# Block ranks of the first batch alone, K block sums between the tiles, mask fills interleaved: an order change in a two-layer kernel on one core

## The chip, the cores and the metric

The kernel runs as one program on one core of one Trainium2 chip. The time is device microseconds of that core. Before the change the median of three runs is 677.49 us (677.4 to 678.2).

A core has five engines with instruction queues of their own: TensorE (PE), VectorE (DVE), ScalarE (ACT), GpSimd (POOL) and SyncE (SP, which here only starts DMAs). Each works through its queue in order. They are tied together by semaphores alone, which the program sets and waits for by hand; no scheduler reorders anything.

## The reference, cut to what matters

Two layers over x of 4 x 256 tokens of width 256, each `x + attention(layernorm(x)) + ffn(layernorm(x))`. Layer 0 is a latent attention with 16 heads and a mixture of 32 experts. Layer 1, in which the change lies, is a block-sparse attention with 16 heads of width 16 and a low-rank mixture of 8 experts:

```
q, k = rope(x @ Wq.T), rope(x @ Wk.T);  v = x @ Wv.T          # 16 heads of 16
km   = k.reshape(B, 8, 32, H, d).mean(axis=2)                 # mean key of each block of 32 tokens
gate = einsum('bshd,bnhd->bhsn', q, km)                       # a score of each token for each block
gate = where(future, -1e30, gate); gate = where(selfb, 1e30, gate)
sel  = the 4 best blocks of each token and head
p    = softmax(where(sel & causal, q k / sqrt(d), -1e30));  o = rmsnorm(p v);  attn = o @ Wo.T

logits = x @ Wg.T;  rw, sel = top_k(softmax(logits), 2);  rw = rw / rw.sum()
base1, base3 = x @ W1.T, x @ W3.T;  a1, a3 = x @ A1[e].T, x @ A3[e].T   (rank 32, each of 8 experts)
for k in (0, 1):                                              # the two chosen experts e
    x2   = silu(base1 + a1[e] @ B1[e].T) * (base3 + a3[e] @ B3[e].T)
    out += (x2 @ W2.T + (x2 @ A2[e].T) @ B2[e].T) * rw[:, k]
```

## The kernel before, in words

Layer 0 fills the first 345 us or so; after it come layer 1's projections (to 379 us), a stretch of preparation (379 to 401 us), the block attention in 16 quads of four heads (401 to 471 us), and then layer 1's feed-forward, almost all TensorE work, to the end. The tokens lie in 8 tiles of 128 (NT), two tiles to a batch (QT), so batch 0 is tiles 0 and 1.

**Projections.** The 8 tiles of q and k are made feature-major, 128 features by 512 tokens (a bank each), in the order PROJECTED: four K tiles, then four Q tiles. For each, VectorE multiplies the bank with the cosines (L1725) and swaps halves by a shuffle (L1728), and GpSimd multiplies the swapped part with the sines (L913). The two are added on VectorE for a K tile (L1734) and on GpSimd for a Q tile (L916). ScalarE copies v and the router's logits out.

**Preparation.** VectorE sums the finished K tiles over blocks of 32 (L1739, one reduction over all 2048 columns), spreads the sums into `kmean` by a product with a head mask (L1745, twice), then takes the largest router logit and the difference from it (L1751, L1753). ScalarE makes the exponentials (L1181), and VectorE ends the router: sum, reciprocal, product, top 8 and their indices, one-hot rows of the first and second expert (L1776), the shares (L1779). In the meantime TensorE does four "low" fills (low-rank parts of x, L2257), then, once q and `kmean` are there, the block scores (L2246, 16 short matmul pairs into banks 0 and 1), four more "low" fills, and eight "mask" fills (L2261) that turn the one-hot rows, which ScalarE has widened to 32 columns per expert (L1213, `expert_of`), into feature-major masks. ScalarE copies every fill out (L1205).

VectorE then takes the block scores of all four batches from the banks (L1784), adds the forced values (L1787), and ranks the blocks: `compare` (L699) writes for a distance d which block beats the one d places on, 0 or 1 in bf16, and `count` (L708, L710) adds these into `rank` and subtracts them from the other side. Batch 0 is counted on VectorE, the rest (tiles 2 to 7) on GpSimd. For the rest VectorE makes comparisons 1 to 3 ahead of the first quad and 4 to 7 behind it. GpSimd waits for all seven, counts three batches, and only then makes the mask difference `step_maskT` (L933).

**Block attention.** For each quad TensorE makes scores (L2274, L2280), VectorE adds the bias of the ranks and takes the minimum in one instruction per part (`masked_minimum`, L1805), ScalarE makes exponentials (`exponents`, L1222), TensorE turns them (L2290), VectorE and ScalarE copy the turned ones out (`odd_probsT`, L1814; `even_probsT`, L1228), and TensorE multiplies them with v. GpSimd prepares the feed-forward's operands meanwhile.

What sets the order around the change is the order in which the code of each engine is written, and these semaphores: `r1_step` and `r1_own` (router, widened rows), `blk_mm`, `blk_step`, `blk_count` (block scores, first ranks), `rest_beats`, `rest_count` (other batches), `kmean_done`, `qkT_out`, `fill_mm`, `fill_out`.

Of the kernel before, what the change touches and what calls it, by code (L numbers as in the profile page):

```python
# [14 lines left out]
ALU = mybir.AluOpType  # L15
ACT = mybir.ActivationFunctionType
AX = mybir.AxisListType
# [285 lines left out]
def program(nc, t, y):  # L303

    ctx = ExitStack()
    with ctx:
# [505 lines left out]
        def _(pool):  # L812
# [96 lines left out]
            for n, (j, c) in enumerate(PROJECTED):  # L909
                plain, turned_ = (rope_tmp[:, n % 4, k, :] for k in range(2))  # L910
                by_batch = turned_.rearrange("p (b s) -> p b s", s=S)
                pool.wait_ge(rope_mul, 2 * n + 2)
                pool.tensor_tensor(by_batch, by_batch, along(heads_rope[:, 1], (1, CH // S)), ALU.mult).then_inc(rope_add, 1)  # L913
                if n >= K_TILES:
                    pool.wait_ge(rope_add, n + 1)
                    pool.tensor_tensor(qkT[:, j, c * CH:(c + 1) * CH], plain, turned_, ALU.add).then_inc(qkT_out, 1)  # L916
# [15 lines left out]
            pool.wait_ge(fill_out, 16)  # L932
            pool.tensor_tensor(step_maskT, second_maskT, first_maskT, ALU.subtract).then_inc(step_mask, 1)  # L933
# [49 lines left out]
        def _(act):  # L983
# [217 lines left out]
            for n, (what, j, h, c) in enumerate(fills()):  # L1201
                act.wait_ge(fill_mm, n + 1)
                cols = slice(c * CH, (c + 1) * CH)
                dst = {"low": am_step[j][:, h, cols], "mask": (first_maskT, second_maskT)[j][:, h, cols]}[what]
                act.activation(dst, bank[4 + n % 4][:, :], ACT.Copy).then_inc(fill_out, 1)  # L1205
                if n == 3:
                    act.wait_ge(qkT_out, len(PROJECTED) - K_TILES)
                    for G in range(2):
                        for par in range(2):
                            own_queries(G, par)  # L1210
                    for k in range(2):
                        act.wait_ge(r1_step, 8 + 2 * NT + k)
                        act.activation(expert_of[k].rearrange("p t (e r) -> p (t e) r", r=R1),  # L1213
                                       along(one_of[k].rearrange("p t e -> p (t e)"), (2, R1)), ACT.Copy).then_inc(r1_own, 1)
                if n == len(fills()) - 4:
                    own_bias(0)
# [30 lines left out]

            own_bias(1)
# [77 lines left out]
        def _(dve):  # L1326
# [393 lines left out]
            for n in range(len(PROJECTED)):  # L1720
# [17 lines left out]
            dve.wait_ge(kmean_done, K_TILES)  # L1738
            dve.tensor_reduce(kblock, qkT[:, 2:4, :].rearrange("p k (n c) -> p k n c", c=CHUNK), AX.X, ALU.add)\  # L1739
                .then_inc(kmean_done, 1)  # L1740
            dve.wait_ge(kmean_done, K_TILES + 1)
# [7 lines left out]

            dve.wait_ge(v_out, NT)  # L1750
            dve.tensor_reduce(max1, logit1, AX.X, ALU.max).then_inc(r1_step, 1)  # L1751
            dve.wait_ge(r1_step, 1)
            dve.tensor_tensor(logit1, logit1, along(max1, (2, E1)), ALU.subtract).then_inc(r1_sub, 1)  # L1753
# [28 lines left out]
            for i in range(2):  # L1782
                dve.wait_ge(blk_mm, 4 * i + 4)
                dve.tensor_tensor(g_b[:, 2 * i:2 * i + 2, :], bank[i][:, :].rearrange("p (b n) -> p b n", b=2),  # L1784
                                  along(table("keep"), (1, 2)), ALU.mult).then_inc(blk_step, 1)
            dve.wait_ge(blk_step, 2)
            dve.tensor_tensor(g_b, g_b, along(table("force"), (1, B)), ALU.add).then_inc(blk_step, 1)  # L1787
            dve.wait_ge(blk_step, 3)
# [5 lines left out]
            for d in (1, 2, 3):  # L1794
                compare(dve, rest_heads, beats_rest, rest_beats, d)
# [54 lines left out]
            for Q in range(QUADS + 4):  # L1850
# [67 lines left out]
        def _(pe):  # L1918
# [316 lines left out]
            for n, (what, j, h, c) in enumerate(fills()):  # L2235
# [4 lines left out]
                if n == 4:  # L2240
                    pe.wait_ge(rope_mul, 2 * len(PROJECTED))
                    pe.wait_ge(kmean_done, K_TILES + 1 + KD)
# [15 lines left out]
                else:  # L2258
                    pe.wait_ge(r1_own, j + 1)
# [161 lines left out]
            pe.wait_ge(blk_step, 2)  # L2421
# [62 lines left out]
```

## Time and profile before

| what | value |
|---|---|
| median of 3 runs | 677.49 us (677.4 to 678.2) |
| profiled execution | 677.35 us, its span 675.3 us |
| TensorE busy | 652.1 us, 97% |
| VectorE, ScalarE, GpSimd busy | 504.9, 412.8, 304.5 us |
| TensorE clock granted | 1.0 of full speed throughout |

The profiled execution's own time is 2.05 us more than its span, which is what lies around the span. The busy share of TensorE says that it works nearly always, but it is an average over stages with different limits, and in the stretch from 379 to 471 us its matmuls are short and wait for others.

### The profile page before, as it was taken

The numbers are of one execution on the slowest core, as the hardware profiler recorded it, in microseconds if no ns is written. First come the engines' busy times: TensorE is split into PE (matmuls) and PEld (weight loads), VectorE is DVE, ScalarE is ACT, GpSimd is POOL, SyncE is SP. The second block draws the span as 40 slices with busy tenths as digits, with TensorE's granted clock in tenths as the row PEclk, the third lists the DMA queues.
The fourth block names the chain that finished last, engine by engine and source line by source line (L and its number), as shares of the span: only waits on it lengthen the run. The fifth ranks groups of instructions, "written<-read, shape, count | busy, mean of one in ns | idle before, by whom it ended". The sixth has DMA issues, their size and how long they took to land.

```text
span 675.3 us, 13767 instructions
## 1 busy us (share of the span) xinstructions
PE 652.1 (97%) x4724; PEld 570.2 (84%) x4724; DVE 504.9 (75%) x1429; ACT 412.8 (61%) x1076; POOL 304.5 (45%) x305
## 2 busy tenths in 40 slices
PE   5999999999999999999999988999999999999998
PEld 3777888898988889888888765656899999999997
DVE  6797876878778786887698998899577745645444
ACT  3766158888888888888864389998554222222221
POOL 1584146455463746452343818999533700400000
PEclk9999999999999999999999999999999999999999
DMA  8903034445536353344560000301100000000000
GB/s 322 373 2 100 3 113 135 153 123 162 159 117 195 100 180 117 116 138 120 210 272 1 1 0 2 111 2 56 72 1 1 2 17 1 1 17 1 1 17 16
DMA packets 26869, 59.65 MB, mean 88 GB/s; under 512 B 3162, under 2 KB 12764, under 8 KB 26416
## 3 DMA queue, kind: packets, MB, share of 16 engines
q1 hardware_dynamic: 23728, 50.58, 22.8%
q0 software_dynamic: 3072, 8.20, 3.6%
q8 instruction: 38, 0.62, 0.4%
q14 instruction: 31, 0.25, 0.1%
HBM read 48.47 MB, written 10.49 MB: 87 GB/s over the span
## 4 chain that ended last, share of the span: by engine, by line
PE 70%; DVE 17%; ACT 8%; issue 3%; DMA 0%; POOL 0%; ACTq 0%; DVEq 0%
PE bank L2321 10%; PE bank L2066 7%; PE bank L2000 6%; PE bank L2057 5%; PE bank L2372 5%; PE bank L2346 5%; ACT sb L1222 4%; PE bank L2086 4%; PE bank L2077 4%; PE bank L2007 4%; PE bank L2128 3%; PE bank L2388 3%; PE bank L2290 2%; PE bank L1940 2%; PE bank L2219 2%
## 5 line engine op out<-in xcount | busy, mean ns | idle before, releaser
L1085 ACT ACTIVATE sb<-bank,sb 128x256 f32<-128x256 f32 x128 | 59.6, 472 | 38.7 <-DVE sb L1586 37.7
L1289 ACT ACTIVATE h_parts<-sb 128x256 fp32r<-128x256 f32 x56 | 23.4, 418 | 76.7 <-DVE sb L1845 45.5
L2066 PE MATMUL bank<-sb 128*128 128x256 f32 x256 | 66.2, 381 | 0.0
L1586 DVE TENSOR_REDUCE sb<-bank 128x2 f32<-128x512 f32 x64 | 43.7, 683 | 27.0 <-PE bank L2066 26.5
L2321 PE MATMUL bank<-rounded,b_hi 128*128 128x256 f32 x224 | 63.0, 281 | 0.0
L2321 PE MATMUL bank<-rounded,b_lo 128*128 128x256 f32 x224 | 63.0, 281 | 0.0
L2321 PE MATMUL bank<-am_lo,b_hi 128*128 128x256 f32 x224 | 62.9, 281 | 0.0
L845 POOL DMA_INDIRECT expert_out<-sb x32 | 33.1, 1034 | 61.3 <-DVE sb L1528 47.4
L1092 ACT ACTIVATE sb<-sb 128x256 f32<-128x256 f32 x128 | 57.8, 504 | 0.1
L1836 DVE TENSOR_TENSOR sb<-sb,bank 128x256 f32<-128x256 f32 x56 | 23.4, 419 | 44.8 <-ACT sb L1246 44.7
L1246 ACT ACTIVATE sb<-bank 128x256 f32<-128x256 f32 x56 | 21.4, 382 | 53.2 <-PE bank L2321 53.2
L2000 PEld LDWEIGHTS bank<-sb 128*128 128x128 f32 (+1 forms) x384 | 46.0, 186 | 5.7 <-DVE sb L1522 3.8
L839 POOL DMA_INDIRECT sb<-rows_x,sb x32 | 32.8, 1026 | 39.0 <-PE bank L2000 19.6
L2000 PE MATMUL bank<-sb 128*128 128x128 f32 (+1 forms) x384 | 49.4, 278 | 0.8 <-DVE sb L1522 0.8
L1597 DVE TENSOR_TENSOR pt_parts<-bank,pt_parts 128x512 fp32r<-128x512 f32 x64 | 43.7, 683 | 8.6 <-ACT pt_parts L1105 7.8
L2066 PEld LDWEIGHTS bank<-sb 128*128 128x128 f32 x256 | 45.2, 190 | 4.8
L1847 DVE TENSOR_TENSOR h_parts<-sb,h_parts 128x256 fp32r<-128x256 f32 x56 | 28.1, 502 | 27.9 <-ACT h_parts L1289 27.9
L1222 ACT ACTIVATE sb<-sb 128x128 f32<-128x128 f32 (+1 forms) x128 | 46.7, 443 | 0.5 <-DVE sb L1805 0.5
L2086 PE MATMUL bank<-pt_parts,xt_parts 128*128 128x256 f32 x256 | 46.0, 301 | 0.0
L2057 PE MATMUL bank<-rounded 128*128 128x512 f32 x160 | 42.7, 399 | 0.2 <-ACT sb L1114 0.2
L2321 PEld LDWEIGHTS bank<-rounded,b_lo 128*128 128x128 f32 x224 | 42.2, 188 | 0.0
L2321 PEld LDWEIGHTS bank<-rounded,b_hi 128*128 128x128 f32 x224 | 42.2, 188 | 0.0
(326 smaller groups left out, 1949.6 us busy)
## 6 DMA issues: line engine op xcount, KB each, us to landing
sb<-in_w_gate_up SPq DMA_DIRECT2D x32, 368.0 KB, 3.0
sb<-in_w_down SPq DMA_DIRECT2D x32, 256.0 KB, 2.7
sb<-in_w_pair SPq DMA_DIRECT2D x8, 704.0 KB, 4.1
expert_out<-sb SPq DMA_DIRECT2D x1, 4096.0 KB, 23.2
sb<-expert_out SPq DMA_DIRECT2D x8, 512.0 KB, 6.9
sb<-in_w SPq DMA_DIRECT2D x1, 1792.0 KB, 12.6
sb<-in_b SPq DMA_DIRECT2D x1, 1792.0 KB, 7.2
sb<-in_sw_up SPq DMA_DIRECT2D x1, 1536.0 KB, 8.8
```

Of the source, the lines that this page charges most:

```text
L1085: act.activation(probs[:, u % 4, q, :], bank[3 + u % 2][:, q * S:(q + 1) * S], ACT.Exp, scale=-1.0, bias=row_min[:, u % 4, q:q + 1], accum ...
L1092: ins = act.activation(probs[:, slot, q, :], probs[:, slot, q, :], ACT.Copy, scale=row_inv[:, slot, q:q + 1])
L1222: act.activation(probs1[:, n % 4, a:b], masked[:, n % 4, a:b], ACT.Exp, scale=-1.0, bias=row_min[:, n % 4, q:q + 1]).then_inc(bl_exp, 1)
L1586: dve.tensor_reduce(row_min[:, u % 4, :], bank[3 + u % 2][:, :].rearrange("p (q n) -> p q n", q=QT), AX.X, ALU.min).then_inc(at_min, 1)
L1597: dve.tensor_tensor(r(probs_lo[:, u % 2]), bank[5 + u % 2][:, :].rearrange("p (a b) -> p a b", a=QT), probs_hi[:, u % 2], ALU.subtract).th ...
L2000: mm = pe.matmul(bank[1][0:n, to:to + P], w_gu[s][:, k, a:a + n], xeT[s][:, k, :], start=(k == 0), stop=(k == KD - 1))
L2057: mm = pe.matmul(where[:, :], r(w[i][:, cols]), r(q[:, half]), start=(n == 0), stop=(n == len(terms) - 1))
L2066: mm = pe.matmul(bank[3 + u % 2][:, q * S:(q + 1) * S], qb[i][:, h, b * S + q * P:b * S + (q + 1) * P], keys[:, h, b * S:(b + 1) * S], sta ...
L2086: mm = pe.matmul(bank[2 + 5 * h][:, 0:S], r(v_parts[:, QT * b + k, :]), r(part[:, u % 2, k, :]), start=(n == 0), stop=(n == len(terms) - 1))
L2321: mm = pe.matmul(dst, lhs, rhs, start=False, stop=(n == len(terms) - 1), skip_group_check=True)
L2346: pe.matmul(dst, r(w[:, 2 * k + j, :]), r(x[:, k, :]), start=(i + j == 0), stop=False, skip_group_check=True)
L2372: mm = pe.matmul(bank[4 + k][:, h * CW:(h + 1) * CW], r(w[:, rows_]), r(x), start=(f + h + i == 0), stop=(f == NF1 - 1 and i == 2), skip_g ...
```

## The change

Seven edits, all of order:

1. The K block sums are four reductions of 512 columns, one behind each of the last four tiles (`n >= K_TILES`), instead of one of 2048 behind all.
2. The router's largest logit and the difference stand ahead of the two `kmean` products.
3. GpSimd multiplies the last tile's sines directly behind those of the tile before; the last Q tile's sum moves from GpSimd to VectorE, behind the `kmean` products.
4. The second expert's widened rows are made by GpSimd instead of ScalarE, and every mask fill waits for both.
5. The fills are four low, then four times one low and two mask. ScalarE's `own_bias(0)` moves from between the last fills to behind them.
6. VectorE takes batch 0's block scores alone (256 columns), forces, compares and counts them; only then the other batches' scores, their forced values and comparison 1. Comparisons 2 to 4 stand behind quad 0, 5 to 7 behind quad 1.
7. GpSimd waits for batch 0's counts before it spreads the shares, and makes `step_maskT` ahead of the counts of the rest; it no longer waits for all seven comparisons at once, since `count` waits for each.

```diff
@@ fills
-            out = [("low", j, h, c) for j in range(2) for h in range(2) for c in range(TOK // CH)]
-            return out + [("mask", k, h, c) for k in range(2) for h in range(2) for c in range(TOK // CH)]
+            low, mask = ([(what, j, h, c) for j in range(2) for h in range(2) for c in range(TOK // CH)]
+                         for what in ("low", "mask"))
+            return low[0:4] + [fill for i in range(4) for fill in (low[4 + i], mask[2 * i], mask[2 * i + 1])]
@@ GpSimd
+            for n in range(len(PROJECTED) - 2):
+                heads_sine(n)
                 if n >= K_TILES:
+                    queries_sum(n)
+            for n in (len(PROJECTED) - 2, len(PROJECTED) - 1):
+                heads_sine(n)
+            queries_sum(len(PROJECTED) - 2)
...
             pool.wait_ge(qkT_out, len(PROJECTED) - K_TILES)
+            pool.wait_ge(r1_step, 9 + 2 * NT)
+            pool.tensor_copy(expert_of[1].rearrange("p t (e r) -> p (t e) r", r=R1),
+                             along(one_of[1].rearrange("p t e -> p (t e)"), (2, R1))).then_inc(r1_own, 1)
             pool.wait_ge(r1_step, 10 + 2 * NT)
+            pool.wait_ge(blk_count, COUNTS)
             for k in range(2):
                 pool.tensor_copy(share_rep[:, k * NT:(k + 1) * NT, :], along(share[:, :, k], (2, P))).then_inc(r1_share, NT)
 
+            pool.wait_ge(fill_out, len(fills()))
+            pool.tensor_tensor(step_maskT, second_maskT, first_maskT, ALU.subtract).then_inc(step_mask, 1)
+
             pool.wait_ge(kmean_set, 5)
-            pool.wait_ge(rest_beats, NB - 1)
             for b in range(1, B):
                 count(pool, QT * H1 * b, slice(QT * H1 * (b - 1), QT * H1 * b), beats_rest, rest_beats, rest_count, COUNTS * (b - 1))
 
-            pool.wait_ge(fill_out, 16)
-            pool.tensor_tensor(step_maskT, second_maskT, first_maskT, ALU.subtract).then_inc(step_mask, 1)
@@ VectorE, in the loop over the projected tiles
+                if n >= K_TILES:
+                    j, c = PROJECTED[n - K_TILES]
+                    blocks = slice(c * CH // CHUNK, (c + 1) * CH // CHUNK)
+                    dve.wait_ge(kmean_done, K_TILES)
+                    dve.tensor_reduce(kblock[:, j - 2, blocks],
+                                      qkT[:, j, c * CH:(c + 1) * CH].rearrange("p (n c) -> p n c", c=CHUNK), AX.X, ALU.add)\
+                        .then_inc(kmean_done, 1)
@@ VectorE, block scores
+            block_scores(0, 1)
+            forced(0, 1, 1)
             dve.wait_ge(blk_step, 2)
             for d in range(1, NB):
                 compare(dve, first_heads, beats_first, blk_beats, d)
 
             dve.wait_ge(kmean_set, 5)
             count(dve, 0, slice(0, QT * H1), beats_first, blk_beats, blk_count, 0)
-            for d in (1, 2, 3):
-                compare(dve, rest_heads, beats_rest, rest_beats, d)
+            block_scores(1, 2)
+            block_scores(2, 4)
+            forced(1, B, 4)
+            dve.wait_ge(blk_step, 5)
+            compare_rest(1)
...
                 if Q == 0:
-                    for d in (4, 5, 6, 7):
-                        compare(dve, rest_heads, beats_rest, rest_beats, d)
+                    compare_rest(2, 3, 4)
+                if Q == 1:
+                    compare_rest(5, 6, 7)
@@ TensorE, mask fills
-                    pe.wait_ge(r1_own, j + 1)
+                    pe.wait_ge(r1_own, 2)
```

`block_scores(a, b)` is L1784's product for batches a to b, with the bank as one input; `forced(a, b, kept)` is L1787's sum for them; `compare_rest` calls `compare` on tiles 2 to 7.

Three places, as the instructions stand in a row. In these rows the first letters are the line, then the operation, output and input, and columns; lines differ between the two kernels because the code above them grew.

VectorE, before, from the last projected tile to the router's softmax (L1739 is the block sums, L1745 the `kmean` products, L1751 and L1753 the largest logit and the difference):

```order
L1725 TENSOR_TENSOR sb<-bank,sb 128x512
L1728 STREAM_SHUFFLE sb<-bank 128x512
L1739 TENSOR_REDUCE sb<-sb 128x64
L1745 TENSOR_TENSOR sb<-sb 128x4x64 x2
L1751 TENSOR_REDUCE sb<-sb 128x8
L1753 TENSOR_TENSOR sb<-sb 128x64
L1757 TENSOR_REDUCE sb<-sb 128x8
```

The same place now (L1753 is now the block sums of one K tile, L1759 and L1761 the largest logit and the difference, L1768 the products, L1775 the last Q tile's sum):

```order
L1738 TENSOR_TENSOR sb<-bank,sb 128x512
L1741 STREAM_SHUFFLE sb<-bank 128x512
L1753 TENSOR_REDUCE sb<-sb 128x16
L1759 TENSOR_REDUCE sb<-sb 128x8
L1761 TENSOR_TENSOR sb<-sb 128x64
L1768 TENSOR_TENSOR sb<-sb 128x4x64 x2
L1775 TENSOR_TENSOR sb<-sb 128x512
L1780 TENSOR_REDUCE sb<-sb 128x8
```

The difference went ahead of the products, and the last Q tile's sum stands between them and the softmax.

GpSimd, before, from the fifth tile's sines to the first counts (L913 sines, L916 Q sums, L921 the ranks' start values, L925 the shares spread, L708 and L710 counts):

```order
L913 TENSOR_TENSOR sb<-sb 128x512 x5
L916 TENSOR_TENSOR sb<-sb 128x512
L913 TENSOR_TENSOR sb<-sb 128x512
L916 TENSOR_TENSOR sb<-sb 128x512
L913 TENSOR_TENSOR sb<-sb 128x512
L916 TENSOR_TENSOR sb<-sb 128x512
L913 TENSOR_TENSOR sb<-sb 128x512
L916 TENSOR_TENSOR sb<-sb 128x512
L921 COPY sb<-sb 128x4x128 x2
L925 COPY sb<-sb 128x1024 x2
L708 TENSOR_TENSOR sb<-sb 128x32x7
L710 TENSOR_TENSOR sb<-sb 128x32x7
```

The same place now (L918 Q sums, L932 start values, L935 the second expert's widened rows, L940 the shares, L943 the mask difference):

```order
L913 TENSOR_TENSOR sb<-sb 128x512 x5
L918 TENSOR_TENSOR sb<-sb 128x512
L913 TENSOR_TENSOR sb<-sb 128x512
L918 TENSOR_TENSOR sb<-sb 128x512
L913 TENSOR_TENSOR sb<-sb 128x512 x2
L918 TENSOR_TENSOR sb<-sb 128x512
L932 COPY sb<-sb 128x4x128 x2
L935 CAST sb<-sb 128x2048
L940 COPY sb<-sb 128x1024 x2
L943 TENSOR_TENSOR masks<-masks 128x2048
L709 TENSOR_TENSOR sb<-sb 128x32x7
L711 TENSOR_TENSOR sb<-sb 128x32x7
```

One Q sum is gone, a cast of 2048 columns has come in, and the mask difference stands ahead of the counts, where it stood behind all three batches.

VectorE, before, from the last count of batch 0 to the first minimum (L699 comparisons of the rest, L1805 the minimum):

```order
L710 TENSOR_TENSOR sb<-sb 128x32
L699 TENSOR_TENSOR sb<-sb 128x672
L699 TENSOR_TENSOR sb<-sb 128x576
L699 TENSOR_TENSOR sb<-sb 128x480
L1805 ISA sb<-bank,sb 128x128
```

The same place now (L1811 is `block_scores`, L1816 `forced`, L700 a comparison, L1844 the minimum):

```order
L711 TENSOR_TENSOR sb<-sb 128x32
L1811 TENSOR_TENSOR sb<-bank,sb 128x256
L1811 TENSOR_TENSOR sb<-bank,sb 128x512
L1816 TENSOR_TENSOR sb<-sb 128x768
L700 TENSOR_TENSOR sb<-sb 128x672
L1844 ISA sb<-bank,sb 128x128
```

Two comparisons left this place, and two products and a forced sum came in.

## Rows read from the trace of the kernel before

**Rows 1.** Stretches; busy us of PE, PE weight loads, VectorE, ScalarE, GpSimd; clock; DMA:
```profile
379.00:399.00 20.00, 18.48 (x127) 14.77 (x129) 18.89 (x66) 13.65 (x24) 9.76 (x9) 1.00 0.01 1
401.00:471.00 70.00, 64.96 (x749) 41.33 (x749) 62.16 (x327) 64.25 (x177) 62.76 (x70) 1.00 0.10 31
480.00:520.00 40.00, 39.21 (x329) 38.62 (x328) 28.75 (x52) 20.23 (x47) 15.03 (x16) 1.00 0.01 1
```

**Rows 2.** The chain of waits at the first minimum: start us, us, what:
```profile
398.98 0.46 DVE sb L699
...
401.67 1.49 ACT sb L1222 x4
```
**Rows 3.** Timeline of VectorE, 378 to 387: start, us, engine, line, operation, [idle before]:
```profile
378.60 0.69 DVE L1725 TENSOR_TENSOR sb<-bank,sb 128x512 f32<-128x512 f32 x1 [0.75 <-PE bank L2219]
...
379.86 2.27 DVE L1739 TENSOR_REDUCE sb<-sb 128x64 f32<-128x2048 f32 x1
382.16 1.08 DVE L1745 TENSOR_TENSOR sb<-sb 128x256 f32<-128x256 f32 x1
383.16 1.52 DVE L1745 TENSOR_TENSOR sb<-sb 128x256 f32<-128x256 f32 x1
...
386.21 0.22 DVE L1757 TENSOR_REDUCE sb<-sb 128x8 f32<-128x64 f32 x1 [0.32 <-ACT sb L1181]
```
**Rows 4.** Timeline of GpSimd, a sine, and the shares:
```profile
382.92 1.48 POOL L913 TENSOR_TENSOR sb<-sb 128x512 f32<-128x512 f32 x1
...
389.77 2.04 POOL L925 COPY sb<-sb 128x1024 f32<-128x1024 f32 x2 [2.85 <-DVE sb L1779]
```
**Rows 5.** Timeline of all engines in the feed-forward, VectorE and GpSimd kept:
```profile
487.57 0.74 POOL L979 TENSOR_TENSOR a_lo<-sb,a_hi 128x256 fp32r<-128x256 f32 x1 [3.35 <-ACT a_hi L1238]
...
487.74 0.85 DVE L1843 TENSOR_TENSOR sb<-sb 128x256 f32<-128x256 f32 x1
...
488.27 1.49 POOL L979 TENSOR_TENSOR w_lo<-sb,w_hi_rest 128x512 fp32r<-128x512 f32 x1
...
488.63 1.40 DVE L1845 TENSOR_TENSOR sb<-sb 128x256 f32<-128x256 f32 x1
```
**Rows 6.** One line of VectorE: shortest/median/longest ns, first and last start:
```profile
L1843 DVE TENSOR_TENSOR sb<-sb x28: 424/426/1057, 487.7 to 665.7; 128x256 f32<-128x256 f32 x28
```
**Rows 7.** Timeline of VectorE, 389 to 405 us:
```profile
389.53 1.28 DVE L1784 TENSOR_TENSOR sb<-bank,sb 128x512 f32<-128x512 f32 x2
390.84 2.03 DVE L1787 TENSOR_TENSOR sb<-sb 128x1024 f32<-128x1024 f32 x1
392.91 1.53 DVE L699 TENSOR_TENSOR sb<-sb 128x224 bf16<-128x224 f32 x7
...
398.98 2.10 DVE L699 TENSOR_TENSOR sb<-sb 128x672 bf16<-128x672 f32 x3
401.00 0.28 DVE L1805 CUSTOM_DVE_ANT_1 sb<-bank,sb 128x128 f32<-128x128 f32 x1
...
403.22 1.43 DVE L699 TENSOR_TENSOR sb<-sb 128x384 bf16<-128x384 f32 x4
404.57 0.55 DVE L1814 COPY sb<-bank 128x384 f32<-128x384 f32 x1
```
**Rows 8.** Timeline of GpSimd, 404 to 447 us:
```profile
404.79 0.60 POOL L708 TENSOR_TENSOR sb<-sb 128x224 f32<-128x224 f32 x1 [12.98 <-DVE sb L699]
...
426.14 4.07 POOL L933 TENSOR_TENSOR masks<-masks 128x2048 bf16<-128x2048 bf16 x1
...
446.35 1.82 POOL L944 CAST b_hi<-sb 128x896 fp32r<-128x896 f32 x2
```
**Rows 9.** Timeline of TensorE, the block scores and the first quad's scores:
```profile
385.95 3.81 PE L2246 MATMUL bank<-sb 128*128 128x128 f32 x32 [1.06 <-POOL sb L916]
...
398.49 0.94 PE L2274 MATMUL bank<-sb 32*128 32x128 f32 x16
```
**Rows 10.** Timeline of ScalarE, the widened rows and the fifth head:
```profile
389.59 3.72 ACT L1213 ACTIVATE sb<-sb 128x2048 bf16<-128x2048 f32 x2
...
406.49 1.48 ACT L1222 ACTIVATE sb<-sb 128x128 f32<-128x128 f32 x4
```

More of the change, by code:

```diff
@@ L908, in _, with heads_sine, queries_sum @@
             pool.wait_ge(ab_in, 32)
-            for n, (j, c) in enumerate(PROJECTED):
-                plain, turned_ = (rope_tmp[:, n % 4, k, :] for k in range(2))
-                by_batch = turned_.rearrange("p (b s) -> p b s", s=S)
+            def heads_sine(n):
+                by_batch = rope_tmp[:, n % 4, 1, :].rearrange("p (b s) -> p b s", s=S)
                 pool.wait_ge(rope_mul, 2 * n + 2)
                 pool.tensor_tensor(by_batch, by_batch, along(heads_rope[:, 1], (1, CH // S)), ALU.mult).then_inc(rope_add, 1)
+            def queries_sum(n):
+                j, c = PROJECTED[n]
+                pool.wait_ge(rope_add, n + 1)
+                pool.tensor_tensor(qkT[:, j, c * CH:(c + 1) * CH], rope_tmp[:, n % 4, 0, :], rope_tmp[:, n % 4, 1, :], ALU.add)\
+                    .then_inc(qkT_out, 1)
+            for n in range(len(PROJECTED) - 2):
+                heads_sine(n)
                 if n >= K_TILES:
-                    pool.wait_ge(rope_add, n + 1)
-                    pool.tensor_tensor(qkT[:, j, c * CH:(c + 1) * CH], plain, turned_, ALU.add).then_inc(qkT_out, 1)
+                    queries_sum(n)
+            for n in (len(PROJECTED) - 2, len(PROJECTED) - 1):
+                heads_sine(n)
+            queries_sum(len(PROJECTED) - 2)
             pool.wait_ge(v_mm, NT)
@@ L1210, in _ @@
                             own_queries(G, par)
[L1211 to L1216, printed above, removed]
+                    act.wait_ge(r1_step, 8 + 2 * NT)
+                    act.activation(expert_of[0].rearrange("p t (e r) -> p (t e) r", r=R1),
+                                   along(one_of[0].rearrange("p t e -> p (t e)"), (2, R1)), ACT.Copy).then_inc(r1_own, 1)
             def exponents(n):
@@ L1246, in activated @@
                 act.activation(f_act[:, m % 2, :], bank[HIDDEN_BANK[n % 4]][:, 0:CW], ACT.Silu).then_inc(f_silu, 1)
+            own_bias(0)
             own_bias(1)
@@ L1781, in _, with block_scores, forced, compare_rest @@
             g_b = score_blk.rearrange("p (b n) m -> p b (n m)", b=B)
[L1782 to L1785, printed above, removed]
+            per_bank = 4 // QT
+            def block_scores(a, b):
+                dve.wait_ge(blk_mm, 4 * (a // per_bank) + 4)
+                src = bank[a // per_bank][:, :].rearrange("p (b n) -> p b n", b=per_bank)
+                at = a % per_bank
+                dve.tensor_tensor(g_b[:, a:b, :], src[:, at:at + b - a, :], along(table("keep"), (1, b - a)), ALU.mult)\
+                    .then_inc(blk_step, 1)
+            def forced(a, b, kept):
+                dve.wait_ge(blk_step, kept)
+                dve.tensor_tensor(g_b[:, a:b], g_b[:, a:b], along(table("force"), (1, b - a)), ALU.add).then_inc(blk_step, 1)
+            def compare_rest(*distances):
+                for d in distances:
+                    compare(dve, rest_heads, beats_rest, rest_beats, d)
+            block_scores(0, 1)
+            forced(0, 1, 1)
             dve.wait_ge(blk_step, 2)
-            dve.tensor_tensor(g_b, g_b, along(table("force"), (1, B)), ALU.add).then_inc(blk_step, 1)
-            dve.wait_ge(blk_step, 3)
             for d in range(1, NB):
@@ L2420, in _ @@
             pe.wait_ge(kmean_set, 3)
-            pe.wait_ge(blk_step, 2)
+            pe.wait_ge(blk_step, 4)
             for Q in range(QUADS + 3):
```

20 lines of the change are left out of this document (11 added, 9 removed).

## The prediction

> **What bounds the kernel now.** I read the page's busy shares first (in the table of the profile before): TensorE works 97% of the span, but that is an average. The stretches [rows 1] show which engine leads where. From 379 to 399 us VectorE is busy 18.89 of 20 us, more than any other; from 401 to 471 us ScalarE 64.25, GpSimd 62.76 and VectorE 62.16 of 70, with TensorE's short matmuls beside them; from 480 us on TensorE alone, 39.21 of 40. The chain of waits [rows 2] shows the hand-over: it runs on VectorE up to the first minimum, at 401.0 us by the timeline [rows 7], and goes over to ScalarE's exponentials at 401.67. So the change acts on a stretch that VectorE bounds, and its worth is read at two points: when the first minimum starts, and when ScalarE gets its fifth head (406.49 us, [rows 10]). What is late there stays late: 16 quads in 70 us are 4.4 us each, of which ScalarE works 4.0, and behind the attention TensorE has no gap to give anything back.
>
> **A hold between VectorE and GpSimd.** The rows say more than durations. In the feed-forward [rows 5] a 256-column VectorE instruction whose inputs both lie in SBUF takes 0.43 us when nothing interferes (the median of its line, [rows 6]); at 487.74 it takes 0.85, beside a GpSimd instruction that ends at 488.31, and at 488.63 it takes 1.40, beside one that ends at 489.76. Each time the excess is what GpSimd had left. It goes both ways: that second GpSimd instruction started at 488.27 while VectorE was still at work. And they take turns: at 488.3 GpSimd's next instruction was issued already, and VectorE, which had waited, came first. The preparation shows the same in the two `kmean` products, 1.08 and 1.52 us for 256 columns [rows 3]: the sine issued at 382.92 takes 1.48 us, as if begun when the first product ended at 383.24, and the second product ends at 384.68, 0.28 behind that sine [rows 4]. It holds for a GpSimd copy: the forced sum of 1024 columns, issued at 390.84, takes 2.03 us, and the shares' copies run until 391.81 [rows 4, 7]. Products with a bank as one input (L1784, 0.64 us per 512 columns beside that copy) are not held, nor are the reductions (L1739), nor the minima.
>
> By the Trainium skill ("SBUF — State Buffer", Who interferes with whom) a VectorE instruction with two SBUF inputs and a GpSimd instruction that reads SBUF exclude each other for the whole of the one that was issued first. Here the trace agrees up to GpSimd instructions of 1.3 us; that it holds for a 4.07 us one, as that page would have it, no row here shows.
>
> The change puts three GpSimd instructions where VectorE has such work: the cast, the shares and the mask difference. So I follow both queues.
>
> **Step 1, to the softmax (edits 1 to 3).** The four reductions cost 2.27 / 4 = 0.57 us each [rows 3]. VectorE had 0.75 us of air in this loop, so the last tile's shuffle ends at about 380.75 instead of 379.9, and the last reduction at 381.3 instead of 382.1: 0.8 won. Then come the largest logit (0.2) and the difference at 381.5, just when GpSimd starts the last sine (1.3 by the one of [rows 4] without its 0.2 of waiting). If that goes first: difference at 382.9, GpSimd's Q sum to 384.2, product 1 (0.43) to 384.6, start values (0.55) to 385.15, product 2 to 385.55, start values to 386.1, and the moved Q sum (0.6) on VectorE to 386.7. If the difference goes first, 386.1. Before, GpSimd's last sum ended at about 385.8, which released the block scores. Middle: 386.4. So the block scores start at 386.5 instead of 385.95 [rows 9], and the softmax's rest at 386.4 instead of 386.21; the exponentials, now early, no longer matter. **+0.2** on VectorE: the 0.8 is used up by two more hand-overs and a sum of 0.6. The one-hot rows were done when L1784 began, 389.5 [rows 7], and are now at 389.7.
>
> **Step 2, ranks of batch 0 (edits 4, 6).** Taken alone, product (0.32, a quarter of the two of L1784) and forced sum (0.43) of 256 columns would end 2.6 us earlier than now. But the cast starts when the one-hot rows end. Its price is not in the trace; the nearest are L944 (1.82 us for 2 x 896 columns, so 2.08 for 2048 [rows 8]) and, at the other end, a bf16 instruction of 2048 columns, 4.07. I take 2.08, since both are one-input casts; half of it, 1.0, is the lower bound. The forced sum then waits until 391.85 and comparisons start at 392.3 instead of 392.91. Comparisons and counts take 398.98 - 392.91 = 6.07 us as before; GpSimd waits meanwhile. Counts end at **398.35, 0.6 earlier**.
>
> **Step 3, to the first minimum (edits 6, 7).** Call this moment T = 398.35. VectorE takes the two products (1.28 us per 1024 columns, so 0.96 for 768, and the waits) and asks for the forced sum of 768 columns (0.9; 1024 took 1.06 behind the copy's end) at T + 1.04. GpSimd, released at T + 0.1, copies shares: first to T + 1.1, then VectorE's forced sum to T + 2.0, the second copy to T + 3.0, comparison 1 (0.8) to T + 3.8 = 402.1. Before, three comparisons (2.10) stood here and GpSimd rested: 401.0 [rows 7]. **+1.1.** TensorE is not late: from its block scores to the first quad's scores it took 398.49 - 385.95 = 12.54 us [rows 9]; with 0.55 of shift and some 0.3 of waiting for the widened rows (ScalarE's 1.86 from 389.7, half of [rows 10], and the cast, both about 391.7, where one low fill covers all but the rest) the quad's scores start at 399.3 and are ready at 400.5. ScalarE's masks and both biases are done by 400.6. The interleaving of edit 5 is thus covered by VectorE; it would cost 0.8 if it were not. The shift of a copy from ScalarE to GpSimd gains ScalarE 1.9 us that nobody waits for.
>
> **Step 4, quad 0 (edit 7).** The mask difference is now next on GpSimd, its masks copied out by 400.0, and it starts when comparison 1 lets go: 402.1 to 406.1 (4.07, [rows 8]). The four heads' minima, not held, take 403.22 - 401.00 = 2.2 us [rows 7], to 404.3. The comparison for distance 2 is then held for 1.8 us. Comparisons 2 to 4 cost 0.7 + 0.6 + 0.5 = 1.8 (the first two and 0.8 make the 2.10 of before), and GpSimd's first two counts (0.60 each, [rows 8], 1.0 in all within this) get in between. The odd copy starts at 406.1 + 2.8 = 408.9; before it stood at 404.57 [rows 7]. Copy 0.5 and fifth minimum 0.6 follow: ScalarE gets head five at 410.0 instead of 406.49 [rows 10]. **+3.5**; the 0.8 us of air which that head had (404.57 + 0.5 + 0.6 = 405.7) is in it. Head three's turn on TensorE waits for the odd copy too, but is not later than this. Comparisons 5 to 7 behind quad 1 (0.9 plus as much hold) lie beside ScalarE's four heads of 2.9 us and its copies.
>
> **What cannot be late next.** GpSimd starts its counts at 406.8 instead of after 404.79, but with the mask difference done: it is through both at about 428.5 instead of 430.2 (426.14 + 4.07, [rows 8]), so the feed-forward's operands come 1.7 us sooner. Batch 1's counts end at about 414.5; its bias is needed at about 419. SP's DMA of b13 follows the counts and has over 10 us.
>
> **Sum.** 677.35 + 3.5 = **680.9 us**; the profiled execution lies 0.14 us under the median, which I leave.
>
> **Rivals.**
> *The mask difference does not hold VectorE* (bf16 in and out, the one shape no row shows). Then quad 0's comparisons take 1.9 from 404.3, odd copy at 406.2, fifth head at 407.3: +0.8, 678.2. For it: nothing held VectorE in the attention beside 4 us instructions; against it: nothing there had two SBUF inputs.
> *Faster: GpSimd's cast and copies do not hold it either*, and the long forced sum of before was slow by itself. Then T is 389.7 + 0.8 + 6.07 = 396.6, forced sum and comparison end at T + 2.7, at 399.3, and TensorE's scores, ready at 400.5 or, with less waiting, sooner, decide as well: first minimum 0.5 to 1.7 us sooner; by its better end 675.7. Against it stand the two ends that fit the copy's end to 0.1 us.
> *Slower still: GpSimd gets the turn* at the second copy (at 390.84 it did, being issued 0.04 us sooner). Then comparison 1 stands behind the mask difference, the first minimum comes at 406, and the first eight heads bear it: +6, 683.4. It decides if VectorE asks for the forced sum after T + 1.1; I have it at 1.04.
> *The cast costs 4 us.* Masks come 2 us later, T is 400.3, first minimum 404: about +5.3.
>
> **How the numbers follow.** The forecast's case 0.58 (679.3 to 682.0, by which GpSimd sine goes first, 0.3 either way, and by the cast from 1.0 to 2.5 us), mask difference not holding 0.14, faster 0.14, the two slower ones 0.10 together, a gain that I have not seen 0.04. What a measurement tells from no change is 0.2%, 1.35 us: 676.1 to 678.8. The faster case straddles that edge (676.9 to 675.7): half of it with the unseen gain is faster, 0.11; the other half and the not-holding case are same, 0.21; the forecast's and the two slower cases are slower, 0.68. A range of 675.9 to 682.6 leaves out the two slowest, the unseen gain and the low end of the faster case: 0.18.
>
> **What would show it.** Right: the mask difference at about 402 to 406 on GpSimd, VectorE's comparison of 576 columns there 2 to 3 us long instead of 0.7, ScalarE idle some 2.5 us before its fifth head, first minimum near 402, attention's end 3 to 4 us later against the same start. Wrong: a forced sum of 256 columns in 0.43 us beside the cast, comparison 2 of 0.7 us beside the mask difference, or a first minimum before 400.5.

## The result and the profile after

The changed kernel takes 679.91 us (median of 8 runs, 678.6 to 680.59), the kernel before 677.49 us in the same comparison. The ratio of the two is 1.0034, with a 95% interval of 1.0024 to 1.0043: **slower by 2.3 us** (1.6 to 2.9), where a change of 0.2% or more can be told from none. The forecast was 680.9. The profiled execution took 680.01 us, its span 678.2.

The stretches of the changed kernel, in the columns of [rows 1] (the clock stands third from the end):

```profile
379.00:399.00 20.00, 17.64 (x117) 14.12 (x115) 19.21 (x70) 13.79 (x25) 9.57 (x9) 1.00 0.00 1
401.00:471.00 70.00, 63.42 (x715) 40.95 (x713) 63.59 (x313) 62.04 (x170) 65.72 (x71) 0.95 0.08 28
```

VectorE still leads up to the first quad. New is the clock: 0.95 on average in the attention, where it was 1.00.

VectorE of the changed kernel, which answers to [rows 3] (first four rows) and [rows 7]:

```profile
381.75 1.37 DVE L1761 TENSOR_TENSOR sb<-sb 128x64 f32<-128x64 f32 x1
...
385.24 1.09 DVE L1775 TENSOR_TENSOR sb<-sb 128x512 f32<-128x512 f32 x1
...
389.94 1.85 DVE L1816 TENSOR_TENSOR sb<-sb 128x256 f32<-128x256 f32 x1
391.83 1.53 DVE L700 TENSOR_TENSOR sb<-sb 128x224 bf16<-128x224 f32 x7
...
397.91 1.02 DVE L1811 TENSOR_TENSOR sb<-bank,sb 128x256 f32<-128x256 f32 x2
398.97 0.96 DVE L1816 TENSOR_TENSOR sb<-sb 128x768 f32<-128x768 f32 x1
399.96 1.57 DVE L700 TENSOR_TENSOR sb<-sb 128x672 bf16<-128x672 f32 x1
401.46 0.28 DVE L1844 CUSTOM_DVE_ANT_1 sb<-bank,sb 128x128 f32<-128x128 f32 x1
...
403.68 4.23 DVE L700 TENSOR_TENSOR sb<-sb 128x576 bf16<-128x576 f32 x3
407.84 0.55 DVE L1853 COPY sb<-bank 128x384 f32<-128x384 f32 x1
```

GpSimd of the changed kernel in the same stretch, which answers to [rows 4] and the first row of [rows 8]:

```profile
389.63 1.89 POOL L935 CAST sb<-sb 128x2048 bf16<-128x2048 f32 x1 [3.84 <-DVE sb L1802]
398.04 2.79 POOL L940 COPY sb<-sb 128x1024 f32<-128x1024 f32 x2 [6.52 <-DVE sb L711]
400.80 4.66 POOL L943 TENSOR_TENSOR masks<-masks 128x2048 bf16<-128x2048 bf16 x1
405.42 1.11 POOL L709 TENSOR_TENSOR sb<-sb 128x224 f32<-128x224 f32 x1
```

Read the two together. The difference of 64 columns takes 1.37 us, since GpSimd's sine got there first (0.23 us in experiment 8, where it didn't). The forced sum of 256 columns ends 0.3 us behind the cast. Comparison 1 ends 0.7 us behind the copies. The mask difference, issued at 400.80, waits for comparison 1 and then works until about 405.45. Quad 0's comparisons take 1.79 us with GpSimd at rest (experiment 5); here they are done only when the odd copy starts, at 407.84. Most of the excess is in the first of them, here taken alone:

```profile
403.68 2.40 DVE L700 TENSOR_TENSOR sb<-sb 128x576 bf16<-128x576 f32 x1
```

The minima between, whose one input is a bank, aren't held by the same mask difference: eight parts take 2.22 us (401.46 to 403.68), as before (401.00 to 403.22).

ScalarE's fifth head, which answers to the last row of [rows 10]:

```profile
408.97 1.49 ACT L1234 ACTIVATE sb<-sb 128x128 f32<-128x128 f32 x4 [1.43 <-DVE sb L1844]
```

It comes 2.48 us later than before, of which 0.21 had come in ahead of 379 us (the low fills start at 379.34 instead of 379.13). Its ninth head is 2.87 us late (414.16 instead of 411.29), the feed-forward's first matmul 2.88, and the span 2.9. The last 0.4 us arose between the fifth and the ninth head, where TensorE was at half clock: the stretch took 5.19 us, against 4.80 before and 4.81 in experiment 1, both at a clock of 1.00. Windows of the changed kernel, columns as in [rows 1]:

```profile
402.00:404.00 2.00, 0.87 (x6) 0.62 (x6) 2.00 (x15) 1.87 (x5) 2.00 (x1) 1.00 0.00 0
404.00:406.00 2.00, 2.00 (x22) 1.01 (x21) 2.00 (x1) 2.00 (x7) 2.00 (x2) 0.66 0.00 0
406.00:408.00 2.00, 1.02 (x5) 0.61 (x3) 2.00 (x4) 0.82 (x2) 1.84 (x3) 0.50 0.02 4
408.00:410.00 2.00, 1.47 (x7) 1.50 (x8) 2.00 (x11) 1.03 (x4) 1.77 (x4) 0.50 0.00 0
410.00:412.00 2.00, 2.00 (x16) 1.83 (x14) 2.00 (x11) 2.00 (x7) 1.29 (x4) 0.64 0.03 8
```

0.50 is the 1.2 GHz level of 2.4. Ahead of the fall TensorE had waited: it was busy 0.84 of 2 us from 398 to 400, and 0.87 from 402 to 404.

### The profile page after: what moved, and what is told of

Same layout as the page of the kernel before. It is cut to its first block, busy times and chain, and to the rows that moved or that the text cites. A ratio compares the mean times of both kernels' runs of the same rounds, so it can differ in the third digit from the quotient of the medians.

```text
span 678.2 us, 13773 instructions
## 1 busy us (share of the span) xinstructions
PE 653.2 (96%) x4724; PEld 571.9 (84%) x4724; DVE 509.5 (75%) x1435; ACT 411.5 (61%) x1075; POOL 306.8 (45%) x305
## 4 chain that ended last, share of the span: by engine, by line
PE 71%; DVE 18%; ACT 6%; issue 4%; DMA 0%; POOL 0%; ACTq 0%; DVEq 0%
PE bank L2361 10%; PE bank L2106 8%; PE bank L2040 7%; PE bank L2097 6%; PE bank L2412 5%; PE bank L2386 5%; PE bank L2126 4%; PE bank L2117 4%; PE bank L2047 4%; ACT sb L1234 3%; PE bank L2168 3%; PE bank L2428 3%; PE bank L2330 2%; PE bank L1980 2%; DVE sb L1713 1%
```

## Experiments

Each ratio is to the kernel before, measured on the same chip. The profiles reach this stage up to 2.6 us apart, so where two are compared I take the time from the start of the one-hot rows to ScalarE's fifth head, the **interval**: 17.28 us before, 19.79 after. The 95% interval of each ratio reaches 0.6 to 0.9 us to either side, so a difference between two experiments is uncertain by about 1 us; where I give one of that size, the profile must bear it out.

**1. The mask difference back behind the counts.**

```diff
-            pool.wait_ge(fill_out, len(fills()))
-            pool.tensor_tensor(step_maskT, second_maskT, first_maskT, ALU.subtract).then_inc(step_mask, 1)
             pool.wait_ge(kmean_set, 5)
             for b in range(1, B): count(...)
+            pool.wait_ge(fill_out, len(fills()))
+            pool.tensor_tensor(step_maskT, second_maskT, first_maskT, ALU.subtract).then_inc(step_mask, 1)
```

> The changed kernel with the mask difference (4.07 us on GpSimd) put back behind the counts; everything else as changed. Hold theory (VectorE work with two SBUF inputs stands still while GpSimd has the ports): the first minimum stays at 401.5 us, the comparisons behind quad 0 are held only by counts of 0.6 us and take about 3 us instead of 4.23, the fifth head comes 1.2 us sooner, and if TensorE's idle gap shrinks the clock does not fall, 0.4 more: 678.2 to 678.8 against 679.9. Rival (the interleaved fills and late masks cost the time, the difference is hidden): no change, 679.9.

Ratio 1.0004 (0.9995 to 1.0012): 2.0 us of the 2.3 are gone. Quad 0's comparisons, in this kernel:

```profile
404.93 2.13 DVE L700 TENSOR_TENSOR sb<-sb 128x576 bf16<-128x576 f32 x3
```

They take 2.13 instead of 4.23 us, the first of them 0.75 instead of 2.40; the interval is 17.75, and the clock of the profile is 1.00. I had expected less, 1.1 to 1.7 us and comparisons of about 3 us. Where the mask difference stands is the main cause.

**2. An instruction that only writes, in the difference's place.** The difference is behind the counts again; two fills of constants stand where it was.

```diff
-            pool.tensor_tensor(step_maskT, second_maskT, first_maskT, ALU.subtract).then_inc(step_mask, 1)
-            pool.wait_ge(kmean_set, 5)
+            for j in range(2):
+                pool.memset(am_first[j], 0.0).then_inc(kmean_set, 1)
+            pool.wait_ge(kmean_set, 7)
             for b in range(1, B): count(...)
+            pool.wait_ge(fill_out, len(fills()))
+            pool.tensor_tensor(step_maskT, second_maskT, first_maskT, ALU.subtract).then_inc(step_mask, 1)
```

> As e1, but two memsets of 2048 columns (about 1.9 us each) stand where the mask difference stood, so that GpSimd is as late as in the changed kernel but reads nothing; the region is overwritten later, so the output is the same. If only instructions that read SBUF hold VectorE: the comparisons behind quad 0 take about 1.9 us, less than in e1, since the counts start later too, the fifth head comes 2 us sooner than in the changed kernel, 677.6 to 678.3. If any GpSimd instruction holds it, or GpSimd's lateness is what costs: as the changed kernel, 679.9.

Ratio 1.0001 (0.9993 to 1.001). GpSimd and VectorE of this kernel:

```profile
400.41 3.55 POOL L944 MEMSET sb<- 128x2048 f32 x2
...
399.60 1.57 DVE L700 TENSOR_TENSOR sb<-sb 128x672 bf16<-128x672 f32 x1
...
403.31 2.19 DVE L700 TENSOR_TENSOR sb<-sb 128x576 bf16<-128x576 f32 x3
```

The two fills take 1.80 us each, the first of them beside comparison 1, which works until 401.17 and takes 1.57 us, as in experiment 1; the second beside nothing of the kind. Neither waited. Quad 0's comparisons, the first begun while the second fill still ran (to 403.96), take 2.19 us, again as in experiment 1 but for 0.06, and that first one takes 0.75 us in both. So it is not that GpSimd is busy, but that it reads SBUF. The Trainium skill ("SBUF — State Buffer", Who interferes with whom) says that a VectorE instruction with two SBUF inputs contends with a GpSimd one that reads SBUF and not with one that only writes it. The runs agree on both counts: the fills held nothing for 3.55 us, and the mask difference, of 4.07 us, for which no row of before could show it, held the first comparison from 403.68 to its own end.

Two limits. The fills end 1.5 us before the mask difference did, so the counts start at 404.04 and not at 405.42, and GpSimd's lateness is only in part the same. And the interval was 18.56 us, 0.8 more than in experiment 1, where I had expected the fifth head 2 us sooner than in the changed kernel: TensorE was at half clock from 404 to 406 (0.50) and in part to 408 (0.66), and ScalarE waited 1.01 us for its matmuls.

**3. The second expert's widened rows back on ScalarE** (edit 4 undone, the cast gone from GpSimd).

```diff
-            pool.wait_ge(r1_step, 9 + 2 * NT)
-            pool.tensor_copy(expert_of[1]..., along(one_of[1]..., (2, R1)))
@@ ScalarE
+                    for k in range(2):
+                        act.activation(expert_of[k]..., ACT.Copy)
@@ TensorE
-                    pe.wait_ge(r1_own, 2)
+                    pe.wait_ge(r1_own, j + 1)
```

> The changed kernel with the second expert's widened rows made by ScalarE again and each mask fill waiting for its own expert's rows. Hold theory: the forced sum of 256 columns takes 0.4 instead of 1.85 us, the counts of batch 0 end 1.4 us sooner (396.5), the first minimum comes at 400.0 to 400.3 (ScalarE's last mask copies and the bias then decide), the mask difference starts at 399.7 and the odd copy of quad 0 is 1.6 us sooner: 678.2 to 678.6. Rival (ScalarE's work was the bound of this stretch): the 1.9 us on ScalarE come back on the path, 680.5 or more.

Ratio 1.0019 (1.001 to 1.0029), against 1.0034: the cast costs about 1.0 us, a little less than expected and a difference that alone is hardly clear of the noise. VectorE of this kernel, the forced sum of 256 columns with GpSimd at rest:

```profile
389.97 0.43 DVE L1814 TENSOR_TENSOR sb<-sb 128x256 f32<-128x256 f32 x1
```

0.43 instead of 1.85, and the interval is 18.37. So the hold of the cast is shown; its price is known only roughly. Beside the mask difference quad 0's comparisons still take 3.75 us.

**4. The kernel before, with only the mask difference moved ahead of the counts.**

```diff
+            pool.wait_ge(fill_out, len(fills()))
+            pool.tensor_tensor(step_maskT, second_maskT, first_maskT, ALU.subtract).then_inc(step_mask, 1)
             pool.wait_ge(kmean_set, 5)
             pool.wait_ge(rest_beats, NB - 1)
             for b in range(1, B): count(...)
-            pool.wait_ge(fill_out, 16)
-            pool.tensor_tensor(step_maskT, second_maskT, first_maskT, ALU.subtract).then_inc(step_mask, 1)
```

> The kernel before with one part of the change alone: the mask difference ahead of the counts, behind the last fill's copy. Hold theory: it runs from 400.9 to 405 us, holds the comparisons that stand behind quad 0 for 1.8 us (odd copy at 406.3 instead of 404.6), fifth head 0.9 us later: 678.2 to 678.8. Rival (GpSimd does not hold a comparison): 677.5 as before, since GpSimd does the same work in another order.

Ratio 1.0014 (1.0005 to 1.0023), that is 0.95 us, as expected. GpSimd, VectorE and ScalarE of this kernel:

```profile
401.44 4.08 POOL L928 TENSOR_TENSOR masks<-masks 128x2048 bf16<-128x2048 bf16 x1 [9.12 <-ACT masks L1205]
403.74 3.08 DVE L699 TENSOR_TENSOR sb<-sb 128x384 bf16<-128x384 f32 x4
407.87 1.49 ACT L1222 ACTIVATE sb<-sb 128x128 f32<-128x128 f32 x4 [0.76 <-DVE sb L1805]
```

The four comparisons of distance 4 to 7 take 3.08 us where they took 1.43 [rows 7]; half of that 1.65 was air of the fifth head (time that VectorE had in hand before ScalarE wanted it), and 0.85 reaches ScalarE. The move alone makes the kernel before slower.

**5. No holds.** The changed kernel with the mask difference behind the counts, the cast on ScalarE, the shares behind comparison 1 and the counts behind comparison 4.

```diff
-            pool.wait_ge(blk_count, COUNTS)
+            pool.wait_ge(rest_beats, 1)
             for k in range(2): pool.tensor_copy(share_rep...)
             pool.wait_ge(kmean_set, 5)
+            pool.wait_ge(rest_beats, 4)
```

> The changed kernel with each long GpSimd read moved off VectorE's path: mask difference behind the counts, second expert's rows on ScalarE (fills wait j + 1), shares copied behind comparison 1 (beside quad 0's minima, whose tiles come from banks), counts of the rest behind four comparisons. Hold theory: forced sums and comparison 1 unheld, VectorE ready at 398.8; TensorE's fills and ScalarE's last copies now end last, first minimum 400.0 to 400.3, quad 0's comparisons 1.9 us; fifth head 0.8 us sooner than in the kernel before: ratio to it 0.9988 (0.998 to 0.9995). Rival (the changed order of fills and sums loses time by itself): 1.000 or more.

Ratio 0.9985 (0.9976 to 0.9994), interval 16.83. What is left of the change is worth 1.0 us once the cast, the shares, the mask difference and the counts are out of VectorE's way: comparison 1 takes 0.86 us and those of quad 0 take 1.79. (The moved Q sum is still held, 1.09 us.) VectorE no longer leads at the first minimum, though:

```profile
399.77 0.29 DVE L1842 CUSTOM_DVE_ANT_1 sb<-bank,sb 128x128 f32<-128x128 f32 x1 [0.84 <-ACT sb L1210]
```

It waits 0.84 us for ScalarE's first bias (L1210), which edit 5 had moved behind the last fills.

**6. No holds, and the preparation too.** As 5; besides, the ranks' start values stand behind the last Q sum on GpSimd, and ScalarE's `own_bias(0)` is between the last fills.

```diff
+            pool.wait_ge(qkT_out, len(PROJECTED) - K_TILES)
             for q in range(QT): pool.tensor_copy(ranks_b[:, q], ...)
-            pool.wait_ge(qkT_out, len(PROJECTED) - K_TILES)
@@ ScalarE, fills
+                if n == len(fills()) - 4:
+                    own_bias(0)
```

> As the one before, and GpSimd writes the ranks' start values (2 copies of 0.6 us) behind the last Q sum instead of ahead of it, and ScalarE makes the first bias between the last fills. Hold theory: the second kmean product and the moved Q sum are not held by the copies, the block scores start 0.5 us sooner (386.0), first minimum 399.4 to 399.7: ratio 0.998 (0.997 to 0.999). Rival (TensorE's fills do not follow the block scores' start): as the kernel before it in this list.

Ratio 0.9969 (0.9957 to 0.9981), faster than both kernels and just beyond the better end of what was expected; its interval overlaps that of experiment 5. VectorE's last Q sum:

```profile
384.79 0.68 DVE L1774 TENSOR_TENSOR sb<-sb 128x512 f32<-128x512 f32 x1
```

0.68 us instead of 1.09. That is ahead of the interval, which went from 16.83 to 16.10 by the bias: VectorE's wait at the first minimum is now 0.38 us, for TensorE's scores.

**7. Experiment 1, and the shares behind comparison 1.**

> The kernel with the mask difference put back, and the shares' copies also moved, behind comparison 1. Hold theory: between the last count and the first minimum 2.7 us instead of 3.55, first minimum 0.8 us sooner: ratio 0.999 to 0.9997 against 1.0004. Rival (TensorE's scores decide the first minimum anyway): no change, 1.0004.

Ratio 1.0012 (1.0002 to 1.0021), where 0.999 to 0.9997 was expected: no gain over experiment 1, though comparison 1 took 0.86 us and the interval of the profile was 17.43, 0.32 shorter. Quad 0's comparisons took 2.60 us with GpSimd's first count beside them, and 9 of 11 executions had a clock of 0.995 to 0.997. Experiment 10 was to tell these apart.

**8. The last Q sum back on GpSimd** (edit 3 undone in the changed kernel).

```diff
-            for n in range(len(PROJECTED) - 2):
+            for n in range(len(PROJECTED)):
                 heads_sine(n)
                 if n >= K_TILES: queries_sum(n)
-            for n in (len(PROJECTED) - 2, len(PROJECTED) - 1):
-                heads_sine(n)
-            queries_sum(len(PROJECTED) - 2)
@@ VectorE
-            dve.tensor_tensor(qkT[:, j, c * CH:(c + 1) * CH], rope_tmp..., rope_tmp..., ALU.add)
```

> The changed kernel with edit 3 alone undone: sines and sums alternate on GpSimd again and the last Q sum is there. My sum for step 1: VectorE's softmax rest 0.2 to 0.4 us sooner without the sum, block scores 0.3 sooner or equal, so 0.2 us: ratio 1.003 (1.002 to 1.004). If edit 3 gained: above 1.004.

Ratio 1.002 (1.0011 to 1.0029): edit 3 costs about 0.9 us, where 0.2 was expected. From the last tile's shuffle to the one-hot rows the changed kernel takes 389.18 - 380.28 = 8.90 us; this one takes 387.29 - 379.26 = 8.03, which bears the size out.

**9. Experiment 6 with edit 3 undone as well**, the edit of 8.

> The kernel of e6 with the last Q tile's sum back on GpSimd (edit 3 undone). If edit 3 costs because VectorE pays 0.68 us for a sum ahead of the softmax while GpSimd is free, this gains up to 0.6 us more on e6's 0.9969: ratio 0.996 (0.995 to 0.9972), forced sum of 256 columns some 0.5 us sooner against the start of the stretch. Rival: GpSimd's sum is held between the two kmean products, the block scores start later and TensorE is the one that is late at the first quad: ratio 0.997 to 0.9985.

Ratio 0.996 (0.9947 to 0.9973), **674.86 us, the fastest kernel here**. VectorE's forced sum, TensorE's shares and ScalarE's first and fifth head in it:

```profile
388.10 0.42 DVE L1807 TENSOR_TENSOR sb<-sb 128x256 f32<-128x256 f32 x1
...
398.79 1.09 PE L2447 MATMUL bank<-sb 128*128 128x128 f32 x8 [0.38 <-POOL sb L934]
398.80 1.49 ACT L1231 ACTIVATE sb<-sb 128x128 f32<-128x128 f32 x4 [0.36 <-DVE sb L1835]
403.62 1.48 ACT L1231 ACTIVATE sb<-sb 128x128 f32<-128x128 f32 x4
```

VectorE waits 0.57 us for the block scores and 0.58 us for the quad's scores, so at both places TensorE is now the later of the two. The interval (17.17) is no measure here, since the first of these waits lies in it; from the last tile's shuffle to the fifth head it is 24.14 us, against 24.39 in experiment 6. The 0.6 us over experiment 6 is as expected, but the two intervals of the ratios overlap, and the profiles show 0.25.

**10. Experiment 7 with the counts behind comparison 4.**

```diff
             pool.wait_ge(kmean_set, 5)
+            pool.wait_ge(rest_beats, 4)
```

> The kernel of e7 (mask difference behind the counts, shares behind comparison 1) with GpSimd's counts waiting for comparison 4. If e7 gave its gain back because the counts start at comparison 2 and hold those behind quad 0 (2.60 us), they take 1.8 us here, ScalarE's fifth head comes 0.5 us sooner against the one-hot rows (16.9 instead of 17.43 us), and the ratio is 0.9995 (0.9985 to 1.0003). Rival: what e7 lost is TensorE's clock, below 1.0 in 9 of its 11 executions, with which the counts have nothing to do: ratio 1.0005 to 1.002 with the same share of such executions.

Ratio 1.0007 (0.9994 to 1.0019): it went the rival's way. The comparisons did shrink to 1.79 us, but the interval grew to 18.17. TensorE of this kernel:

```profile
399.43 0.94 PE L2314 MATMUL bank<-sb 32*128 32x128 f32 x16 [1.18 <-ACT masks L1220]
400.30 0.61 PE L2320 MATMUL bank<-cb 128*128 128x256 bf16 x4
402.31 1.97 PE L2456 MATMUL bank<-sb 128*128 128x128 f32 x8 [1.41 <-POOL sb L940]
```

and its windows:

```profile
398.00:400.00 2.00, 0.82 (x21) 0.64 (x18) 1.93 (x4) 1.97 (x5) 0.00 (x0) 1.00 0.00 0
400.00:402.00 2.00, 0.91 (x12) 0.31 (x4) 1.97 (x9) 0.35 (x2) 0.78 (x1) 0.93 0.02 4
402.00:404.00 2.00, 1.69 (x8) 1.69 (x9) 2.00 (x12) 1.68 (x6) 1.24 (x2) 0.50 0.00 0
```

The matmuls that turn the shares (L2456) stand in TensorE's queue between the first quad's scores and its turned probabilities. With the copies behind comparison 1 TensorE waits 1.41 us for them, and then does these eight at half clock in 1.97 us (1.04 in the changed kernel), and VectorE's odd copy waits 0.47 us for TensorE, where in experiment 7 it had none to wait for. On average the executions sort by clock: the three at 0.995 took 679.41 to 679.67 us, the three at 0.997 took 678.21 to 678.52, the one at 0.999 took 677.85, the five at 1.0 took 675.77 to 678.56. In 7 the same wait is 1.40 us, but its profile kept a clock of 1.00, and there the interval is shorter than in experiment 1. So the wait alone did not make the fifth head late; in the profile of 10 the half clock behind it did. That the clock is also what experiment 7 lost is likely and not shown: its nine executions below 0.999 took 0.8 us longer on average than its two at 1.0, and spread from 676.17 to 679.82. In 5, 6 and 9 the wait is 0.57, 0.58 and 0.38, and the clock never fell below 0.999.

## Why the forecast held, step by step

The mechanism was right: the mask difference ran from about 401.4 to 405.45 us on GpSimd, and VectorE's comparison of 576 columns took 2.40 us beside it, inside the 2 to 3 us named as the sign. The sizes in steps 1 to 4 were off, most of them on the high side.

- **Step 1 (+0.2 forecast).** The shuffle moved by 0.85 us, the sine went first, and the moved sum took 1.09 us instead of 0.6, held by the start values. Yet against its own start VectorE was 0.24 us early at the one-hot rows, and the block scores were 0.32 late. The small sum hides two larger terms of opposite signs, which the forecast had as 0.8 won and 1.0 used up by two more hand-overs and the moved sum. By experiment 8 edit 3 costs 0.9 us, so that edits 1 and 2 must have won about 1.1; no run has these two alone.
- **Step 2 (T = 398.35).** T was 397.91. The cast took 1.89 us (2.08 assumed) and began when the rows were there; the forced sum ended behind it, as forecast, but by 0.27 us and not by its whole 0.43. The same 0.27 and 0.28 stand in [rows 5] (490.03 - 489.76 and 488.59 - 488.31), where the forecast read the excess as all that GpSimd had left; it is 0.15 us less. The cast's hold shows in experiment 3.
- **Step 3 (first minimum T + 3.8, +1.1).** It was T + 3.55, 401.46: +0.46, or +0.25 without the 0.21 from ahead of the stretch. The order was as forecast: first copy, forced sum, second copy, comparison 1. The forced sum was asked for at T + 1.06 (forecast 1.04) and done at T + 2.02 (forecast 2.0). Behind it the second copy ended 0.08 us sooner than forecast, and comparison 1 let the first minimum start 0.63 us behind that copy instead of 0.8. The most mis-sized terms of the sum are the 0.44 us in T and the 0.4 in step 4.
- **Step 4 (+3.5 at the fifth head).** From first minimum to odd copy it was 6.38 us instead of 6.8: behind the mask difference's end (about 405.45, where GpSimd's first count is issued) the comparisons and the counts between them took 2.4 us instead of 2.8. The fifth head was +2.48.
- **Not foreseen: TensorE's clock.** It goes with 0.4 us between the fifth and ninth head of the profile. Of the changed kernel's 8 executions the five at 0.995 to 0.997 took 679.81 to 680.59 us, the three at 0.999 or more 678.6 to 679.31. Executions of the kernel before were at 0.999 or 1.0 in 73 of the 78 that ran beside the experiments.
- **The sum.** Forecast +3.5. In the profile the sizes of steps 2 to 4 took 1.1 us off and the clock put 0.4 back, to a span 2.9 us longer. The medians differ by less, +2.3 by the ratio, and the changed kernel's three executions without a fallen clock by about 1.5.

The rivals fell. That the mask difference doesn't hold: the comparisons of 4.23 us. That the cast and copies don't: the forced sum of 0.43 us in experiment 3, and comparison 1 of 0.86 us in experiment 5. That GpSimd gets the turn at the second copy: comparison 1 came first, as the turns of [rows 5] had it. The cast of 4 us: 1.89.

The ledger by experiments, each against the changed kernel and uncertain by about 0.9 us: mask difference 2.0 us (1), cast and its place 1.0 (3), edit 3 0.9 (8). The first two add up to more than the 2.3 lost, as they should: with them and with the shares and counts moved as well the change gains 1.0 us (5), so these four are worth 3.3 together. Edits 1, 2 and 6 and the interleaving of edit 5 were tested in no run of their own. Alone in the kernel before the mask difference costs only 0.95 (4), where 0.8 us of air stood behind it. In experiment 1 that air is down to 0.1 us (the odd copy starts at 406.99, 0.5 + 0.6 us of copy and minimum follow, the fifth head comes at 408.19), since quad 0's comparisons take 2.13 us there and 1.43 before. This is worked out from the traces; no run shows it alone.

## What to carry to other kernels

An instruction moved to an idle engine isn't free because that engine is idle: ask what it reads, and which two-input instruction of VectorE is next while it runs. A long GpSimd instruction belongs where VectorE reads banks or reduces (the minima kept their 2.22 us beside the mask difference, the block sums of 512 columns their 0.67 us beside the sines), and it pays to let it wait by one more semaphore until then: the change was +2.3 us as it stands and -1.0 with four pieces of GpSimd's work moved. When a copy is put off, look for the matmuls that wait for it in TensorE's queue, since in experiment 10 such a wait, of 1.4 us, was followed by half clock.

## What the runs showed of the hardware

- VectorE's instructions with two SBUF inputs and GpSimd's that read SBUF hold each other, in both directions, for GpSimd instructions of up to 4.1 us and also where GpSimd's inputs are bf16; filling with constants holds nothing (3.55 us, experiment 2), and a minimum with one input from a bank isn't held (0.28 and 0.41 us for 128 and 256 columns beside the mask difference).
- Where both had an instruction waiting, the one that had waited longer came next, in every such place that these rows show: in the changed kernel first copy, forced sum (asked for at 398.97), second copy (issued at 399.02), comparison 1 (399.96), mask difference (400.80).
- TensorE's granted clock fell to 0.50, 1.2 GHz, for some 3 to 7 us in the first quads of four profiles (the changed kernel, experiments 2, 8 and 10), behind waits of 1.2 to 2.0 us. The fall isn't certain: the profiles of experiments 1, 3 and 7 had waits of 1.0 to 1.5 us as well and kept 1.00.
- What it costs stays open. Executions with a mean clock of 0.995 or 0.997 took longer on average than those of the same kernel at 0.999 or 1.0 by 1.1 us in the changed kernel, 1.9 in experiment 10, 0.5 to 0.9 in experiments 2, 3, 7 and 8 and 0.2 in experiment 1; in experiment 4 two such executions were 0.8 us shorter. Whether the clock alone makes the difference, or the executions in which it falls differ in another way too, no run shows.
